# Vision-tower kernel: each half of the edge convolution in front of a value group, the second half of the keys one group later

## The chip, the cores and the metric

The kernel runs on one core of one Trainium2 chip. The metric is the device time of one execution in microseconds, the median of the runs. TensorE (PE) does matmuls and its own weight loads (PEld); VectorE (DVE), ScalarE (ACT) and GpSimd (POOL) do the elementwise work; SyncE's queue (SP) issues the DMAs. Each engine works through its own instructions in the order in which they are written, and semaphores hold it where it needs another's result.

## The reference

One transformer layer over 32 grey edge images of 256 rows; each row of an image is a token of 256 values, with a class token ahead (257 tokens). Cut to what matters:

```python
gray  = einsum('bchw,c->bhw', x, w)                       # 32 images 256x256
edge  = (|conv(gray, scharr_x)| + |conv(gray, scharr_y)|) / 2
h     = concat([cls, edge], axis=1)                       # 257 tokens
q,k,v = split(layernorm(h) @ w_qkv + b_qkv)               # 16 heads of 16
att   = softmax(where(causal, q @ k.T / 4, -inf))
h     = h + (att @ v) @ w_out + b_out
h     = h + fake_quant_ffn(layernorm(h))                  # 704 wide, gate and up, int8 style
```

The attention stage fills about the first 880 us, the feed-forward stage the rest. The change touches the attention stage only.

## The kernel before, in words

The attention stage is a software pipeline over images. Step n works on up to seven images at once: the grey sum of image n, the convolution, layer norm and transposes of image bC = n-2, the q, k, v projections of bP = n-3, the scores of bS = n-4, softmax and values of bT = n-5, and the output projection of bO = n-6. Steps 8 to 29 are a hardware loop in pairs; the others are written out. In every step each engine has one fixed order by hand; nothing else schedules. The names on PE, each a line of `step`:

- `scores(u)`, u = 0 to 7: scores of two heads into SX (L939, L942), so that DVE can take row maxima (`maxima`, L706 and L708). SX has one buffer, so `scores(u)` waits for the maxima of u-1.
- `scores_t(b, par, u)`: the scores again, transposed, into ST (L956); ACT takes the exponential into `prob` (L542).
- `outputs(b, par, g)`, g = 0 to 3: the value group, probabilities of four heads times v, into G (L975), in 32-column tiles. It waits for `sel_done`: POOL's `select` (L449, then the causal mask L451) on the same four heads.
- `edges(t)`, t = 0, 1: half of the convolution into the PSUM bank M1 (L994), also in 32-column tiles. ACT takes the absolute value (`absolute`, L572), DVE goes on (`edge_tile`, L734).
- `keys(m)` into M0 or M1 (L1007), `queries(m)` into M0 (L1018). ACT copies each result twice (L552 and L554, L563 and L565).
- `spread_rec` (L1055): spreads the reciprocals of the softmax sums over G. It waits for the DMA `rec<-den` (L375), which SP issues after the four `yun<-yun` DMAs.
- `turn_max`: turns the maxima into M1 (L1046); DVE copies them (L723), and a DMA brings them to `qst`.

POOL's step, for the part that matters (it is written once and the same before and after):

```python
select(bT, 1)
...                                   # L462, a small copy
wait(pool, kx_ready, bP, 4, 4)        # both halves of the keys copied by ACT
nc.gpsimd.tensor_tensor(kr, kx, kpart[0], subtract)       # L466
select(bT, 2)
...
```

So the selection for `outputs(2)` stands on POOL behind L466, and L466 waits for ACT's copies of `keys(1)`. Later in the same step stand L471 (keys), L475 (queries), L480 to L483 (layer norm) and `select(bT, 3)`, which `outputs(3)` needs.

Of the kernel before, what the change touches and what calls it, by code (L numbers as in the profile page):

```python
# [73 lines left out]
def vit_tower(nc, x, cls_tok, scharr, w_qkv, b_qkv, w_out, b_out, clip_x, clip_down,  # L74
# [8 lines left out]
    with ctx:  # L83
# [423 lines left out]
        def _(act):  # L507
# [22 lines left out]
            def step(n, par):  # L530
                bC, bP, bS, bT = n - 2, n - 3, n - 4, n - 5

                def exponential(b, u):
                    if valid(b):
                        g = u // 2
                        wait(act, sT_done, b, 8, u + 1)
                        if u % 2 == 0:
                            if g >= 2:
                                wait(act, pv_done, b, 4, g - 1)
                            else:  # L540
                                wait(act, pv_done, b - 1, 4, 3 + g)
                        nc.scalar.activation(prob[:, g % 2, 2 * (u % 2):2 * (u % 2) + 2, 0:QEND],  # L542
                                             ST[:, :, 0:QEND], ACT.Exp).then_inc(exp_done, 1)

                def keys(m):
                    if valid(bP):
                        wait(act, k_done, bP, 2, m + 1)
                        if m == 0:
                            wait(act, k_rest, bP - 1, 1, 1)
                            wait2(act, kst_loaded, bP - 1, par, 96)  # L550
                        bias = bqk[:, KC + m:KC + m + 1]
                        nc.scalar.activation(kpart[:, 0, m, 1:T], M[m][:, 0:IMG], ACT.Identity, bias=bias  # L552
                                             ).then_inc(kx_ready, 1)
                        nc.scalar.activation(kx[:, m, 1:T], M[m][:, 0:IMG], ACT.Identity, bias=bias  # L554
                                             ).then_inc(kx_ready, 1)

                def queries(m):
                    if valid(bP):
                        wait(act, q_done, bP, 2, m + 1)
                        if m == 0:  # L560
                            wait(act, q_rest, bP - 1, 1, 1)
                            wait2(act, qst_loaded, bP - 1, par, 96)
                        nc.scalar.activation(qpart[:, 0, m, :], M[0][:, 0:IMG], ACT.Identity,  # L563
                                             bias=bq4[:, m:m + 1], scale=HD ** -0.5).then_inc(qx_ready, 1)
                        nc.scalar.activation(qx[:, m, :], M[0][:, 0:IMG], ACT.Identity,  # L565
                                             bias=bq4[:, m:m + 1], scale=HD ** -0.5).then_inc(qx_ready, 1)

                def absolute(t):
                    if valid(bC):
                        wait(act, conv_done, bC, 2, t + 1)  # L570
                        wait(act, ln1, bC - 1, LN, 2 * t + 1)
                        nc.scalar.activation(habs[:, t, :, :], M[1][:, :].rearrange("p (f w) -> p f w", f=2),  # L572
                                             ACT.Abs, scale=0.5).then_inc(abs_done, 1)
# [7 lines left out]
                                       ).then_inc(yun_ready, 1)  # L581

                exponential(bT, 3)
                absolute(0)
                keys(0)
                exponential(bT, 4)
                keys(1)
                exponential(bT, 5)
                queries(0)
                absolute(1)  # L590
                exponential(bT, 6)
                if valid(bP):
                    wait(act, k_rest, bP, 1, 1)
                    nc.scalar.copy(kpart[:, 1, :, 1:T], kr[:, :, 1:T]).then_inc(k_mid, 1)  # L594
# [279 lines left out]
        def _(pe):  # L874
# [49 lines left out]
            def step(n, par):  # L924
# [20 lines left out]
                def scores_t(b, par_, u):  # L945
                    if valid(b):
                        if u >= 1:
                            wait(pe, exp_done, b, 8, u)
                        else:
                            wait(pe, exp_done, b - 1, 8, 8)  # L950
                        if u % 4 == 0:
                            wait(pe, m_loaded[u // 4], b, 16, 16)
                        for r in range(2):
                            i = 2 * u + r
                            for k in range(KT):
                                last = mm(ST[0:KEYS[k], r, QAT[k]:QAT[k] + QN[k]],  # L956
                                          kst[par_][:, i, KFIRST[k]:KFIRST[k] + KEYS[k]], qst[par_][:, i, Q0[k]:IMG],
                                          start=True, stop=True)
                        last.then_inc(sT_done, 1)

                def outputs(b, par_, g):
                    if valid(b):
                        wait(pe, sel_done, b, 4, g + 1)
                        if g % 2 == 0:
                            wait(pe, yun_ready, b - 1, 2, g // 2 + 1)
                        if g == 2:
                            wait(pe, yn_done, b - 1, 1, 1)
                        if g == 0:
                            wait2(pe, v_placed, b, par_, 16)
                            wait(pe, v_ready, b, 1, 1)  # L970
                            wait(pe, v_first, b, 2, 2)
                        for k in range(KT):
                            for j in range(4):
                                o = G[32 * j:32 * j + 32, g // 2, IMG * (g % 2) + Q0[k]:IMG * (g % 2) + IMG]
                                last = mm(o, vaug[par_][0:KEYS[k], k, head_at(4 * g + j), :],  # L975
                                          prob[0:KEYS[k], g % 2, j, QAT[k]:QAT[k] + QN[k]],
                                          start=k == 0, stop=k == KT - 1)
                        last.then_inc(pv_done, 1)

                def edges(t):  # L980
                    if valid(bC):
                        if t == 0:
                            wait(pe, gst_loaded, bC, 96, 96)
                            wait(pe, msplit, bT, 2, 2)
                            if ends:
                                wait(pe, v_first, bS, 2, 2)
                                wait(pe, abs_done, bC - 1, 2, 2)
                        else:
                            wait(pe, kx_ready, bP, 4, 4)
                            if ends:  # L990
                                wait(pe, abs_done, bC, 2, 1)
                        for f in range(2):
                            for j in range(4):
                                last = mm(M[1][32 * j:32 * j + 32, IMG * f:IMG * f + IMG], cw[:, f, :],  # L994
                                          gst[:, 4 * t + j, :], start=True, stop=True)
                        last.then_inc(conv_done, 1)

                def keys(m):
                    if valid(bP):
                        if m == 0:  # L1000
                            wait(pe, xT_ready, bP, 1, 1)
                        else:
                            wait(pe, abs_done, bC, 2, 1)
                            if ends:
                                wait(pe, msplit, bT, 2, 2)
                        for c in range(KC):
                            last = mm(M[m][:, 0:IMG], wqkv[:, c, D + P * m:D + P * m + P], xT[:, c, 1:T],  # L1007
                                      start=c == 0, stop=c == KC - 1)
                        last.then_inc(k_done, 1)
# [40 lines left out]
                def spread_rec():  # L1050
                    if valid(bO):
                        wait(pe, rec_moved, bO, 16, 16)
                        wait(pe, yun_ready, bO, 2, 2)
                        for c in range(KC):
                            last = mm(G[:, 1, IMG * c:IMG * c + IMG], sel[0:H, P * c:P * c + P],  # L1055
                                      rec[:, :], start=True, stop=True)
                        last.then_inc(rec_spread, 1)
# [28 lines left out]
                    pe.wait_ge(w_sd, 1)  # L1086
                scores(0)
                scores_t(bT, odd, 3)
                edges(0)
                keys(0)  # L1090
                scores(1)
                scores_t(bT, odd, 4)
                outputs(bT, odd, 1)
                keys(1)
                scores(2)
                scores_t(bT, odd, 5)
                spread_rec()
                queries(0)
                edges(1)
                scores(3)  # L1100
                scores_t(bT, odd, 6)
                outputs(bT, odd, 2)
                queries(1)
                turn_max(0)
# [546 lines left out]
```

## Time and profile before

| | us |
|---|---|
| median of 3 runs (1167.91 to 1173.79) | 1169.92 |
| the profiled execution | 1166.12 |
| its span in the trace | 1164.4 |
| PE busy | 949.2 |
| DVE busy | 806.9 |
| ACT busy | 686.8 |
| POOL busy | 537.5 |

The busy times are sums over the whole span. Two stages stand in it: up to about 880 us the attention pipeline, in which PE is busy 461.10 of the 500 us from 300 to 800, and then the feed-forward stage, in which DVE is the busiest. PE's granted clock is at its full level of 2.4 GHz in the first of these stretches (the profile's 1.00). A step of the pipeline is seen as the distance between two `edges(0)`.

### The profile page before, as it was taken

What the parts mean: (1) busy time and instruction counts of PE and PEld (TensorE: products, weight loads), DVE (VectorE), ACT (ScalarE), POOL (GpSimd) and SP (SyncE); (2) the same over time, 40 slices, a digit from 0 to 9 for tenths busy, and PEclk for the clock granted to TensorE, in tenths of its full rate; (3) what the DMA queues carried; (4) which work ended last, traced back from release to release, by engine and by line L of the source; (5) the groups of instructions that cost most, each with busy time, mean ns of one, the idle gap of its engine ahead of it and who ended that gap; (6) DMA issues with size and microseconds to landing.
All of it is one profiled execution on the core that took longest, in us unless ns stands there. A gap on an engine that the chain in (4) does not pass through costs nothing. (4 is left out here: it accounts for less than half of the span.)

```text
span 1164.4 us, 28062 instructions
## 1 busy us (share of the span) xinstructions
PE 949.2 (82%) x9584; PEld 681.1 (58%) x9584; DVE 806.9 (69%) x1969; ACT 686.8 (59%) x1171; POOL 537.5 (46%) x685
## 2 busy tenths in 40 slices
PE   2268899989989999899999999989988458885665
PEld 1045666666766767676676766767666333332544
DVE  1735566777776677777767777776666359998687
ACT  0154666666666666666666666666554237785785
POOL 5243555566556555655656565556443242220000
PEclk9988999999999999999999999999998769998888
DMA  3854455555555556555455655554322005501874
GB/s 86 233 133 112 126 138 152 149 133 148 149 133 129 137 154 150 138 150 143 126 135 148 154 135 150 148 131 105 101 62 62 12 1 199 199 1 50 271 231 137
DMA packets 156101, 152.90 MB, mean 131 GB/s; under 512 B 28263, under 2 KB 152458, under 8 KB 153994
## 3 DMA queue, kind: packets, MB, share of 16 engines
q1 hardware_dynamic: 156042, 152.14, 48.2%
q8 instruction: 34, 0.56, 0.2%
q14 instruction: 25, 0.20, 0.1%
HBM read 67.49 MB, written 28.35 MB: 82 GB/s over the span
## 5 line engine op out<-in xcount | busy, mean ns | idle before, releaser
L542 ACT ACTIVATE prob<-ST 128x772 f32<-128x772 f32 x256 | 209.2, 817 | 149.2 <-PE ST L956 143.9
L706 DVE TENSOR_REDUCE mneg<-SX 128x2 f32<-128x258 f32 x256 | 107.5, 420 | 212.3 <-PE SX L942 211.7
L939 PE MATMUL SX<-kst,qst 96*128 96x257 bf16 (+1 forms) x1024 | 159.9, 250 | 19.1 <-DMA qst<-qpart 10.4
L708 DVE TENSOR_REDUCE mneg<-SX 128x2 f32<-128x514 f32 x256 | 174.0, 680 | 0.0
L956 PE MATMUL ST<-qst,kst 98*128 98x256 bf16 (+2 forms) x1536 | 138.7, 223 | 15.5 <-DMA qst<-mpart 15.2
L942 PE MATMUL SX<-mask_s,ident_b 128*128 128x256 bf16 x512 | 142.4, 278 | 0.0
L451 POOL TENSOR_SCALAR_AFFINE_SELECT prob<-prob 128x1016 f32<-128x1016 f32 x128 | 142.2, 1111 | 0.0
L956 PEld LDWEIGHTS ST<-qst,kst 98*128 98x128 bf16 x1536 | 120.9, 99 | 33.8 <-DMA qst<-mpart 12.7
L939 PEld LDWEIGHTS SX<-kst,qst 96*128 96x128 bf16 x1024 | 91.7, 99 | 64.3 <-issue 28.2
L975 PE MATMUL G<-prob,vaug 128*32 128x256 f32 (+2 forms) x3072 | 117.3, 282 | 14.2 <-POOL prob L451 13.2
L975 PEld LDWEIGHTS G<-prob,vaug 128*32 128x32 f32 x3072 | 83.5, 111 | 48.1 <-POOL prob L451 19.7
L994 PE MATMUL M<-gst,cw 102*32 102x256 f32 x1024 | 71.1, 396 | 26.2 <-DMA gst<-gray_dram 17.1
L499 POOL TENSOR_TENSOR gray<-xin 128x512 f32<-128x512 f32 x32 | 40.5, 1267 | 90.4 <-ACT xin L620 90.4
L471 POOL TENSOR_TENSOR kpart<-kqr,kpart 128x512 bf16<-128x512 f32 x32 | 37.0, 1156 | 95.2 <-ACT kpart L594 95.2
L1368 ACT ACTIVATE work<-GU,gsc 128x512 f32<-128x512 f32 x96 | 65.4, 685 | 23.7 <-PE GU L1570 23.4
L1622 PE MATMUL GU<-wdT,hq 128*128 128x256 bf16 x384 | 54.5, 311 | 30.3 <-ACT hq L1396 30.3
L466 POOL TENSOR_TENSOR kqr<-kqr,kpart 128x512 f32<-128x512 f32 x32 | 37.0, 1157 | 86.0 <-ACT kqr L554 86.0
L449 POOL TENSOR_TENSOR tick<-half 128x2 f32<-128x2 f32 x128 | 29.9, 234 | 99.9 <-ACT prob L542 99.8
L1007 PE MATMUL M<-xT,wqkv 128*128 128x256 f32 x256 | 73.1, 409 | 0.0
L1570 PE MATMUL GU<-work,wgT 128*128 128x512 bf16 x192 | 58.5, 387 | 17.0 <-ACT work L1354 10.9
L1018 PE MATMUL M<-xT,wqkv 128*128 128x256 f32 x256 | 72.3, 404 | 0.0
L620 ACT ACTIVATE xin<-xin 128x512 f32<-128x512 f32 x96 | 53.1, 620 | 23.8 <-DMA xin<-in_x 23.8
(226 smaller groups left out, 1991.8 us busy)
## 6 DMA issues: line engine op xcount, KB each, us to landing
kst<-kpart SPq DMA_DIRECT2D x192, 128.5 KB, 2.5
xin<-in_x SPq DMA_DIRECT2D x96, 256.0 KB, 4.0
gst<-gray_dram SPq DMA_DIRECT2D x96, 256.0 KB
qst<-qpart SPq DMA_DIRECT2D x192, 128.0 KB, 2.4
h_dram<-hb SPq DMA_DIRECT2D x8, 1280.0 KB, 4.6
gray_dram<-gray SPq DMA_DIRECT2D x64, 128.0 KB, 2.7
result<-oy SPq DMA_DIRECT2D x32, 256.0 KB, 3.4
hb<-h_dram SPq DMA_DIRECT2D x5, 1280.0 KB, 6.5
```

Source lines behind the costliest of these rows:

```text
L451: nc.gpsimd.affine_select(p, p, [[0, 4], [-1, 2], [1, P - 1]], ALU.is_ge, 0.0, base=1, channel_multiplier=-1).then_inc(sel_done, 1)
L542: nc.scalar.activation(prob[:, g % 2, 2 * (u % 2):2 * (u % 2) + 2, 0:QEND], ST[:, :, 0:QEND], ACT.Exp).then_inc(exp_done, 1)
L706: nc.vector.tensor_reduce(mneg[:, 0, u // 4, 0, at], SX[:, :, S0:S0 + P + 1], AX.X, ALU.max, negate=True)
L708: nc.vector.tensor_reduce(mneg[:, 1, u // 4, 0, at], SX[:, :, S1:S1 + T], AX.X, ALU.max, negate=True).then_inc(max_done, 1)
L939: mm(SX[:, r, at:at + k], qst[par][0:SR, 2 * u + r, P * t:P * t + P], kst[par][0:SR, 2 * u + r, 0:k], start=t == 1, stop=False)
L942: last = mm(o, ident_b[:, :], mask_s[:, :, :], start=False, stop=True)
L956: last = mm(ST[0:KEYS[k], r, QAT[k]:QAT[k] + QN[k]], kst[par_][:, i, KFIRST[k]:KFIRST[k] + KEYS[k]], qst[par_][:, i, Q0[k]:IMG], start=Tru ...
L975: last = mm(o, vaug[par_][0:KEYS[k], k, head_at(4 * g + j), :], prob[0:KEYS[k], g % 2, j, QAT[k]:QAT[k] + QN[k]], start=k == 0, stop=k == ...
L994: last = mm(M[1][32 * j:32 * j + 32, IMG * f:IMG * f + IMG], cw[:, f, :], gst[:, 4 * t + j, :], start=True, stop=True)
L1007: last = mm(M[m][:, 0:IMG], wqkv[:, c, D + P * m:D + P * m + P], xT[:, c, 1:T], start=c == 0, stop=c == KC - 1)
L1018: last = mm(M[0][:, 0:IMG], wqkv[:, c, P * m:P * m + P], xT[:, c, 1:T], start=c == 0, stop=c == KC - 1)
L1368: nc.scalar.activation(silu[0:IW[k], j % NSI, :], GU[k % 3][0:IW[k], 0, :], ACT.Silu, scale=gsc[0:IW[k], k:k + 1]).then_inc(silu_done, 1)
```

## The change

On PE `edges(0)` goes from in front of `keys(0)` to in front of `outputs(1)`, `edges(1)` from behind `queries(0)` to in front of `outputs(2)`, and `keys(1)` from behind `outputs(1)` to behind `spread_rec`, in front of `queries(0)`. ACT's copies go into the matching order. POOL's, DVE's and SP's orders stay. The waits inside the functions stay too.

```diff
 # ACT
                 exponential(bT, 3)
-                absolute(0)
                 keys(0)
                 exponential(bT, 4)
+                absolute(0)
+                exponential(bT, 5)
                 keys(1)
-                exponential(bT, 5)
                 queries(0)
+                exponential(bT, 6)
                 absolute(1)
-                exponential(bT, 6)
 # PE
                 scores(0)
                 scores_t(bT, odd, 3)
-                edges(0)
                 keys(0)
                 scores(1)
                 scores_t(bT, odd, 4)
+                edges(0)
                 outputs(bT, odd, 1)
-                keys(1)
                 scores(2)
                 scores_t(bT, odd, 5)
                 spread_rec()
+                keys(1)
                 queries(0)
-                edges(1)
                 scores(3)
                 scores_t(bT, odd, 6)
+                edges(1)
                 outputs(bT, odd, 2)
                 queries(1)
                 turn_max(0)
```

PE before, in a step of the loop, from the end of `outputs(1)` (L975) over `keys(1)` (L1007) to `spread_rec` (L1055), `queries(0)` (L1018) and `edges(1)` (L994):

```order
L975 MATMUL G<-prob,vaug 32x1 x4
L1007 MATMUL M<-xT,wqkv 128x256 x2
L939 MATMUL SX<-kst,qst 128x257
...
L956 MATMUL ST<-qst,kst 128x1
L1055 MATMUL G<-rec,sel 128x256 x2
L1018 MATMUL M<-xT,wqkv 128x256 x2
L994 MATMUL M<-gst,cw 32x256 x8
L939 MATMUL SX<-kst,qst 128x257
```

PE now, in the same stretch of a step, from `edges(0)` and `outputs(1)` on:

```order
L994 MATMUL M<-gst,cw 32x256 x8
L975 MATMUL G<-prob,vaug 32x256 x4
L975 MATMUL G<-prob,vaug 32x129 x4
L975 MATMUL G<-prob,vaug 32x1 x4
L939 MATMUL SX<-kst,qst 128x257
...
L956 MATMUL ST<-qst,kst 128x1
L1055 MATMUL G<-rec,sel 128x256 x2
L1007 MATMUL M<-xT,wqkv 128x256 x2
L1018 MATMUL M<-xT,wqkv 128x256 x2
L939 MATMUL SX<-kst,qst 128x257
```

`keys(1)` has moved behind one `scores`, one `scores_t` and `spread_rec`; the convolution stands directly in front of the value group.

ACT before, in a step of the loop, from the copies of `keys(0)` (out of M0) on:

```order
L552 ACTIVATE kpart<-M0,bqk 128x256
L554 ACTIVATE kqr<-M0,bqk 128x256
L542 ACTIVATE prob<-ST 128x2x386
L552 ACTIVATE kpart<-M1,bqk 128x256
L554 ACTIVATE kqr<-M1,bqk 128x256
L542 ACTIVATE prob<-ST 128x2x386
L563 ACTIVATE qpart<-M0,bq4 128x256
L565 ACTIVATE kqr<-M0,bq4 128x256
L572 ACTIVATE habs<-M1 128x512
```

ACT now, in the same stretch:

```order
L552 ACTIVATE kpart<-M0,bqk 128x256
L554 ACTIVATE kqr<-M0,bqk 128x256
L542 ACTIVATE prob<-ST 128x2x386
L572 ACTIVATE habs<-M1 128x512
L542 ACTIVATE prob<-ST 128x2x386
L552 ACTIVATE kpart<-M1,bqk 128x256
L554 ACTIVATE kqr<-M1,bqk 128x256
L563 ACTIVATE qpart<-M0,bq4 128x256
L565 ACTIVATE kqr<-M0,bq4 128x256
```

The copies of `keys(1)` (out of M1) stand one exponential later, and directly in front of those of `queries(0)`.

## Rows read from the trace of the kernel before

**Rows 1.** The page, part 1: busy us (share of span) and instructions.

```profile
PE 949.2 (82%) x9584; PEld 681.1 (58%) x9584; DVE 806.9 (69%) x1969; ACT 686.8 (59%) x1171; POOL 537.5 (46%) x685
```

**Rows 2.** Waits of PE, 250 to 750 us: us in total, times, longest.

```profile
PE M L1046 <- DVE mneg L715: 11.8, 19, 0.8
PE G L975 <- POOL prob L451: 7.9, 18, 0.6
PE M L994 <- DVE mpart L723: 7.5, 19, 0.6
```

**Rows 3.** Timeline of PE, one step: start, us, line, tile, count [idle before, releaser].

```profile
399.60 0.53 PE L956 MATMUL ST<-qst,kst 98*128 98x256 bf16 x6
...
400.34 1.07 PE L994 MATMUL M<-gst,cw 102*32 102x256 f32 x16 [0.22 <-DVE mpart L723]
401.34 1.13 PE L1007 MATMUL M<-xT,wqkv 128*128 128x256 f32 x4
...
403.42 0.90 PE L975 MATMUL G<-prob,vaug 128*32 128x256 f32 x24
404.25 1.13 PE L1007 MATMUL M<-xT,wqkv 128*128 128x256 f32 x4
405.22 0.33 PE L939 MATMUL SX<-kst,qst 96*128 96x257 bf16 x2
...
405.78 0.53 PE L956 MATMUL ST<-qst,kst 98*128 98x256 bf16 x6
406.24 1.13 PE L1055 MATMUL G<-rec,sel 16*128 16x256 f32 x4
407.29 1.13 PE L1018 MATMUL M<-xT,wqkv 128*128 128x256 f32 x4
408.36 1.07 PE L994 MATMUL M<-gst,cw 102*32 102x256 f32 x16
...
410.39 0.90 PE L975 MATMUL G<-prob,vaug 128*32 128x256 f32 x24
...
417.62 0.90 PE L975 MATMUL G<-prob,vaug 128*32 128x256 f32 x24 [0.62 <-POOL prob L451]
...
426.12 1.07 PE L994 MATMUL M<-gst,cw 102*32 102x256 f32 x16 [0.58 <-DVE mpart L723]
```

**Rows 4.** Timeline of POOL in the same step.

```profile
399.53 1.27 POOL L499 TENSOR_TENSOR gray<-xin 128x512 f32<-128x512 f32 x1 [2.69 <-ACT xin L620]
...
402.25 1.11 POOL L451 TENSOR_SCALAR_AFFINE_SELECT prob<-prob 128x1016 f32<-128x1016 f32 x1
...
406.33 1.16 POOL L466 TENSOR_TENSOR kqr<-kqr,kpart 128x512 f32<-128x512 f32 x1 [2.27 <-ACT kqr L554]
...
407.78 1.11 POOL L451 TENSOR_SCALAR_AFFINE_SELECT prob<-prob 128x1016 f32<-128x1016 f32 x1
...
413.30 1.16 POOL L475 TENSOR_TENSOR qr<-kqr,qpart 128x512 f32<-128x512 f32 x1 [0.17 <-ACT kqr L565]
414.66 0.71 POOL L480 TENSOR_TENSOR rs<-ve,half 128x2 f32<-128x2 f32 x1 [0.20 <-DVE ve L748]
```

**Rows 5.** Timeline of ACT in the same step.

```profile
405.79 0.47 ACT L554 ACTIVATE kqr<-M,bqk 128x256 f32<-128x256 f32 x1
```

**Rows 6.** Timeline of SP's queue, in two steps of the loop and in a late one.

```profile
403.86 0.58 SPq L375 DMA_DIRECT2D rec<-den  x1
...
429.48 0.58 SPq L375 DMA_DIRECT2D rec<-den  x1
...
866.33 0.58 SPq L375 DMA_DIRECT2D rec<-den  x1
```

**Rows 7.** Timeline of PE in that late step.

```profile
868.23 1.13 PE L1055 MATMUL G<-rec,sel 16*128 16x256 f32 x4 [0.86 <-DMA rec<-den]
...
871.27 0.90 PE L975 MATMUL G<-prob,vaug 128*32 128x256 f32 x24
```

**Rows 8.** Timeline of DVE in the step of rows 3.

```profile
400.55 0.67 DVE L708 TENSOR_REDUCE mneg<-SX 128x2 f32<-128x514 f32 x1
```

## The prediction

> **What bounds the kernel now.** I read the page's busy times first [rows 1]: PE is the busiest engine at 82% of the span, but no engine is at its limit over the whole span. The next view was PE's waits in the middle of the attention stage [rows 2]. The reader is to see that they are short and many: each of the three largest comes about once in each of the 19 or so steps of that stretch, 0.4 to 0.6 us at a time. So a step is a ring of handovers in which PE is nearly always working and is held several times for a few tenths. In such a ring time taken out of PE counts only up to the next handover that is already tight, and time added to another engine's chain counts from where that chain's slack ends. So I followed one step through the timelines of PE, POOL, ACT and SP [rows 3 to 6]. It lasts 25.78 us, from `edges(0)` at 400.34 to the next at 426.12.
>
> Three handovers matter, in order.
>
> First, `outputs(1)` at 403.42. POOL's mask L451 started at 402.25 and took 1.11, so it ended at 403.36, and PE started 0.06 later. POOL had been at work without a pause worth the name since 399.53, when ACT's L620 released it [rows 3, 4]. So PE stood right at POOL's heel, and can't come earlier by being faster itself.
>
> Second, `outputs(2)` at 410.39. Its mask started at 407.78 and ended at 408.89, so there were 1.50 us between the end of the mask and its use, of which 0.06 are the handover: 1.44 us of slack. POOL had idled 2.27 us before L466, released by ACT's L554, the second copy of `keys(1)` [rows 3 to 5]. The chain is `keys(1)` on PE at 404.25, ACT's L554 from 405.79 to 406.26, POOL's L466 at 406.33, mask ended at 408.89, value group possible at 408.95. That is 4.70 us from the start of `keys(1)` to the earliest `outputs(2)`.
>
> Third, `outputs(3)` at 417.62, for which PE did idle 0.62 us on POOL. That POOL chain hangs on `queries(1)` and on `turn_max(0)`: L475 idled 0.17 for the copy of the queries and L480 0.20 for DVE's statistics, which follow the copy of the turned maxima [rows 3, 4]. Both stand behind `outputs(2)` on PE. So a delay of `outputs(2)` arrives at `outputs(3)` whole.
>
> **The change part by part.** No instruction is added or removed, and no wait. All costs are of position.
>
> `edges(0)` leaves the place in front of `keys(0)`. It held PE for 1.00 us (400.34 to 401.34), with 0.22 us idle in front in this step and 0.58 in the next, 7.5 us over 19 times [rows 2, 3]. That idle time goes, since by its new place DVE's copy has long been made. `keys(0)` would start 0.46 after the start of `scores_t` at 399.60 (the distance from 405.78 to 406.24), at 400.06, and `scores(1)` 0.97 later (the distance 404.25 to 405.22), at 401.03 [rows 3]. DVE's maxima of `scores(0)` end at 400.55 + 0.67 = 401.22 [rows 8], so here a new wait of 0.2 to 0.3 us is late next. Then come 0.56 for `scores(1)` (405.22 to 405.78), 0.46 for `scores_t`, `edges(0)` at about 402.3 and `outputs(1)` at the earliest at 403.2 to 403.4, depending on whether a convolution in front of a value group takes as little as a value group (0.83, from 403.42 to 404.25) or as much as now (1.00); no row shows that pair. In either case it is POOL's 403.36 that decides, and `outputs(1)` stays at 403.42. Gain so far: nothing.
>
> `keys(1)` leaves the place behind `outputs(1)`. `scores(2)` then starts at 403.42 + 0.83 = 404.25, `scores_t` at 404.81, and `spread_rec` could start at 405.27. It now started at 406.24. But the DMA that it waits for was issued at 403.86 in this step [rows 6]. How long this DMA takes to release PE is seen in the late step where PE did wait for it: issued at 866.33, `spread_rec` at 868.23, so 1.90 us [rows 6, 7]. That makes 405.76, a new wait of 0.49 us. The queue itself doesn't gain: its DMAs are released through DVE's copy of the maxima at the step's start, and SP's order is the old one. `keys(1)` follows 1.05 later (406.24 to 407.29), at 406.81 instead of 404.25. With the 4.70 us of the chain, `outputs(2)` can start at 411.51 instead of 410.39: 1.12 us later. In the following step the DMA is issued 25.62 us later (429.48) while the step is 25.78 long, so the loss there is 0.96. The two kinds of step alternate, and the mean is **1.04 us a step**.
>
> PE itself would not be late. `keys(1)` and `queries(0)` take 0.97 each, `scores(3)` 0.56, `scores_t` 0.46 and `edges(1)` 0.83 to 1.00, about 3.9 in all, so PE is ready for `outputs(2)` at 406.81 + 0.97 + 0.97 + 0.56 + 0.46 + about 0.9 = 410.7. It waits 0.8 us there for POOL. If the DMA doesn't hold `spread_rec`, `outputs(2)` is at 405.27 + 1.05 + 4.70 = 411.02, still 0.63 late; that is the lower bound of this term (0.47 in the other kind of step, mean 0.55). The upper bound is reached if ACT and POOL have to queue more than now: ACT's copies of `queries(0)` now follow directly behind those of `keys(1)`, and `absolute(1)` falls between the next exponential and the copy L594; none of these stands in front of L554, so I allow another 0.5 us, 1.5 in all.
>
> `edges(1)` moves behind `scores_t`. Its successors (the absolute value, DVE's `edge_tile`, then the copy of the turned maxima) have until `turn_max(0)`, two groups later, now also 1 us later. `edges(1)` at about 409.8 ends by 410.9, ACT's L572 behind it by 411.7, `turn_max(0)` comes at 411.51 + 0.83 + 0.97 = 413.31. I cost it at nothing; what hides it is `outputs(2)` and `queries(1)`.
>
> Switches between 32-column and 128-column groups get fewer. `queries(0)` in front of `edges(1)` takes 1.07 (407.29 to 408.36), `keys(1)` in front of `scores(2)` 0.97, so such a border costs about 0.10 [rows 3]. The Trainium skill ("TensorEngine Tiling (Array Packing)", Key Properties) says that changing the tiling mode drains the engine. The trace agrees with its 0.10 us at the border. Four borders a step go, since each half of the convolution now shares its way in and out with a value group: 0.4 us of PE's time a step. By that rule alone the kernel would get faster. I give the 0.4 us no value in the sum, because it lies in front of POOL's release at `outputs(1)` and at `outputs(2)`.
>
> **The sum.** Steps 6 to 33 have all stages, 28 in number: 28 x 1.04 = 29.1 us. In step 34 there is no convolution, but the keys move too: `spread_rec` at 868.23, `keys(1)` 1.05 later at 869.28, `outputs(2)` at 873.98 instead of 871.27 [rows 7], 2.7 us. Steps 3 to 5, where the weights are prepared, and the steps behind 34, which have no keys, I put at 0, with 3 us either way. The feed-forward stage isn't touched. Together +31.8 us. The profiled execution took 1166.1 (span 1164.4), so it would be 1197.9; it lay 3.8 us below the median of the runs, 1169.9, and with the same 31.8 the median is **1201.7**. A measurement of this kernel can tell about 0.5% (6 us) from no change, and this is 2.7%.
>
> **The rivals.**
> - PE sets the step, and the ring gives way (faster). Then the idle time at `edges(0)` (7.5 / 19 = 0.39 us) and the four borders (0.4) are gained: 0.8 x 28 = 22 us, 1148; with the borders alone 0.4 x 28 = 11 us, 1159. For it: PE's 82%. Against it: POOL's mask is tight at `outputs(1)` already, and the distance `keys(1)` to `outputs(2)` shrinks on PE while the chain through ACT and POOL keeps its length. It decides if the chain from `keys(1)` through ACT and POOL were shorter than PE's own 3.9 us between the two groups, and POOL released `outputs(1)` earlier. Chance 0.09. The case of the borders alone is the one of the Trainium skill's page named above.
> - The delay at `outputs(2)` is absorbed later, at the places where PE waits now (0.62 at `outputs(3)`, 0.6 at `turn_max(1)` by the row of L1046 [rows 2]). For it: the waits are there. Against it: they are chains that start at PE's own late groups. Time: 1170 plus what is left, 1166 to 1176. Chance 0.07.
> - The DMA holds nothing, only POOL's chain does: 28 x 0.55 + 2.7 = 18 us, 1188. Chance 0.17.
> - More is queued than I see (1.5 us a step): 28 x 1.5 + 2.7 = 45 us, 1215. Chance 0.12.
> - My forecast, both holds as worked out, 1201.7: chance 0.55.
>
> **How the numbers follow.** Faster by over 0.5%: 0.09. Within 0.5%: 0.07. Slower by over 0.5%: 0.55 + 0.17 + 0.12 = 0.84. The range takes in the forecast, the case without the DMA and most of the case above: 1182 to 1214.
>
> **What would show it.** Right: POOL's idle time before L466 grows from 2.3 to nearly 5 us; PE's waits show `outputs` on L451 with 0.8 us more a step (from 7.9 us in 500 to over 20), `spread_rec` on the `rec<-den` DMA with about 0.5 us a step, and a new short one of L939 on DVE's L708; the waits of L994 on L723 are gone; a step is about 26.8 us. Wrong: `outputs(2)` shows no idle time on POOL, or it does and the step is still 25.8 us or less, so that a later wait gave it back.

## The result and the profile after

| | before | after |
|---|---|---|
| median of 4 runs, us | 1171.86 | 1209.13 (1203.52 to 1216.36) |
| profiled execution, us (span) | 1166.12 (1164.4) | 1203.52 (1201.8) |

The ratio is 1.031, with a 95% interval of 1.026 to 1.036. The forecast was 1201.7 us, a ratio of 1.027.

The waits of PE between 250 and 750 us, in the kernel after (us in total, times, longest):

```profile
PE ST L956 <- DMA qst<-mpart: 19.1, 37, 1.2
PE M L1046 <- DVE mneg L715: 15.2, 18, 1.0
PE G L975 <- POOL prob L451: 13.0, 24, 0.6
PE SX L939 <- DVE mneg L708: 5.6, 18, 0.5
PE G L1055 <- DMA rec<-den: 2.8, 10, 0.3
```

In the kernel before, the first of these stood fourth, behind the three of [rows 2]:

```profile
PE ST L956 <- DMA qst<-mpart: 5.9, 18, 0.5
```

Against [rows 2] three things are to be seen. The wait of L994 on L723 is gone and a short one of L939 on L708 has come, both as forecast. POOL's mask is waited for longer, 13.0 instead of 7.9 us, but not the 20 and more that I expected. And the largest wait is one of which the prediction said nothing: `scores_t` on the DMA `qst<-mpart`, twice a step.

One step on PE, after (start, us; idle time before and its releaser in brackets):

```profile
412.56 0.54 PE L956 MATMUL ST<-qst,kst 98*128 98x256 bf16 x6 [0.27 <-DMA qst<-mpart]
413.03 1.07 PE L994 MATMUL M<-gst,cw 102*32 102x256 f32 x16
413.92 0.87 PE L975 MATMUL G<-prob,vaug 128*32 128x256 f32 x24
415.29 0.53 PE L956 MATMUL ST<-qst,kst 98*128 98x256 bf16 x6
416.12 1.12 PE L1055 MATMUL G<-rec,sel 16*128 16x256 f32 x4 [0.29 <-DMA rec<-den]
417.17 1.13 PE L1007 MATMUL M<-xT,wqkv 128*128 128x256 f32 x4
418.14 1.03 PE L1018 MATMUL M<-xT,wqkv 128*128 128x256 f32 x4
419.56 0.53 PE L956 MATMUL ST<-qst,kst 98*128 98x256 bf16 x6
420.02 1.07 PE L994 MATMUL M<-gst,cw 102*32 102x256 f32 x16
421.68 0.90 PE L975 MATMUL G<-prob,vaug 128*32 128x256 f32 x24 [0.58 <-POOL prob L451]
...
428.07 0.54 PE L956 MATMUL ST<-qst,kst 98*128 98x256 bf16 x6 [0.59 <-DMA qst<-mpart]
428.90 0.90 PE L975 MATMUL G<-prob,vaug 128*32 128x256 f32 x24 [0.29 <-POOL prob L451]
```

POOL in the same step, after:

```profile
419.25 1.16 POOL L466 TENSOR_TENSOR kqr<-kqr,kpart 128x512 f32<-128x512 f32 x1 [5.32 <-ACT kqr L554]
...
420.51 1.11 POOL L451 TENSOR_SCALAR_AFFINE_SELECT prob<-prob 128x1016 f32<-128x1016 f32 x1
```

SP's queue in the same step, after:

```profile
414.13 0.58 SPq L375 DMA_DIRECT2D rec<-den  x1
...
421.15 2.09 SPq L392 DMA_DIRECT2D gst<-gray_dram  x6
424.43 0.70 SPq L360 DMA_DIRECT2D qst<-mpart  x1
...
426.11 3.82 SPq L403 DMA_DIRECT2D kst<-kpart  x6
```

The forecast chain is there: L466 idles 5.32 us for the copies of `keys(1)` (2.27 in [rows 4]), the mask ends at 421.62 and `outputs(2)` starts 0.06 later after 0.58 us idle. Beside it stands the second thing: SP issues the `gst` loads only when `edges(1)` has ended (420.02 + 1.07, issue at 421.15), the small `mpart` DMA follows at 424.43, and `scores_t(bS, 0)` can start only at 428.07, 3.64 us after its issue.

To compare kernels I measured the start of each group of a step from the start of DVE's L723 in front of it (the copy for the second half of the maxima). These are medians over 10 to 20 steps of the loop, most between 300 and 760 us, worked out from the start times in each trace. Where two kinds of step alternate, other stretches give medians that differ by up to 0.2 us, and in the row of `edges(1)` alone by up to 0.5:

| us from L723 | spread_rec | edges(1) | outputs(2) | gst issued | mpart issued | scores_t(bS,0) | outputs(3) | step |
|---|---|---|---|---|---|---|---|---|
| before | 6.41 | 8.53 | 10.56 | 9.68 | 13.31 | 16.66 | 17.61 | 25.64 |
| after | 5.87 | 9.78 | 11.44 | 10.94 | 14.19 | 18.01 | 18.71 | 26.83 |
| keys(1) moved alone | 5.87 | 8.99 | 11.44 | 10.14 | 14.19 | 17.17 | 18.53 | 26.58 |
| both edges moved alone | 6.78 | 9.82 | 10.71 | 10.98 | 13.44 | 18.33 | 18.80 | 27.24 |
| edges(0) alone | 6.78 | 8.89 | 10.93 | 10.05 | 13.68 | 16.94 | 18.01 | 26.08 |
| edges(1) alone | 6.35 | 9.40 | 10.29 | 10.58 | 13.02 | 17.86 | 18.33 | 27.48 |
| after, small gst | 5.88 | 9.79 | 11.45 | 10.94 | 14.20 | 17.10 | 18.53 | 26.54 |
| after, select first | 5.88 | 9.79 | 10.67 | 10.94 | 13.40 | 18.51 | 18.98 | 27.40 |
| after, small gst and select first | 5.88 | 9.79 | 10.67 | 10.94 | 13.40 | 16.31 | 17.75 | 25.75 |

Where the 37.4 us between the two spans lie is seen from `spread_rec`: its first group (step 6), the one in step 34 and its last (step 37). Before, beside [rows 7], it stands at

```profile
147.23 1.13 PE L1055 MATMUL G<-rec,sel 16*128 16x256 f32 x4
...
931.28 2.07 PE L1055 MATMUL G<-rec,sel 16*128 16x256 f32 x4 [8.96 <-DMA rec<-den]
```

and after at

```profile
146.94 1.13 PE L1055 MATMUL G<-rec,sel 16*128 16x256 f32 x4 [0.42 <-DMA rec<-den]
...
901.10 1.13 PE L1055 MATMUL G<-rec,sel 16*128 16x256 f32 x4 [1.42 <-DMA rec<-den]
907.13 0.90 PE L975 MATMUL G<-prob,vaug 128*32 128x256 f32 x24 [0.38 <-POOL prob L451]
...
971.25 2.07 PE L1055 MATMUL G<-rec,sel 16*128 16x256 f32 x4 [8.96 <-DMA rec<-den]
```

From step 6 to step 34 it took 721.0 us before (147.23 to 868.23) and 754.2 after (146.94 to 901.10): 33.2 us more, 1.18 a step. From there to the last it took 63.1 before and 70.2 after, 7.1 more; the mean granted clock in these two stretches was 0.83 before and 0.75 after. All the rest is 2.9 us less.

### The profile page after: what moved, and what is told of

It is laid out like the page before. It is cut to its first block and busy times, and to the rows that moved or that the text cites. A ratio compares the mean times of both kernels' runs of the same rounds, so it can differ in the third digit from the quotient of the medians.

```text
span 1201.8 us, 28084 instructions
## 1 busy us (share of the span) xinstructions
PE 948.6 (79%) x9584; PEld 682.7 (57%) x9584; DVE 819.5 (68%) x1969; ACT 685.3 (57%) x1171; POOL 532.3 (44%) x685
## 5 line engine op out<-in xcount | busy, mean ns | idle before, releaser
L939 PE MATMUL SX<-kst,qst 96*128 96x257 bf16 (+1 forms) x1024 | 160.3, 251 | 24.2 <-DVE mneg L708 11.6
L708 DVE TENSOR_REDUCE mneg<-SX 128x2 f32<-128x514 f32 x256 | 173.9, 679 | 0.0
L956 PE MATMUL ST<-qst,kst 98*128 98x256 bf16 (+2 forms) x1536 | 139.0, 223 | 39.6 <-DMA qst<-mpart 39.3
L956 PEld LDWEIGHTS ST<-qst,kst 98*128 98x128 bf16 x1536 | 118.7, 99 | 63.7 <-DMA qst<-mpart 29.8
L451 POOL TENSOR_SCALAR_AFFINE_SELECT prob<-prob 128x1016 f32<-128x1016 f32 x128 | 142.3, 1112 | 0.0
L975 PE MATMUL G<-prob,vaug 128*32 128x256 f32 (+2 forms) x3072 | 116.8, 282 | 23.7 <-POOL prob L451 23.1
L975 PEld LDWEIGHTS G<-prob,vaug 128*32 128x32 f32 x3072 | 86.2, 112 | 72.1 <-POOL prob L451 40.6
L939 PEld LDWEIGHTS SX<-kst,qst 96*128 96x128 bf16 x1024 | 89.9, 99 | 63.9 <-DVE mneg L708 35.8
L466 POOL TENSOR_TENSOR kqr<-kqr,kpart 128x512 f32<-128x512 f32 x32 | 37.1, 1158 | 170.1 <-ACT kqr L554 170.1
L994 PE MATMUL M<-gst,cw 102*32 102x256 f32 x1024 | 71.0, 396 | 17.9 <-DMA gst<-gray_dram 17.1
L449 POOL TENSOR_TENSOR tick<-half 128x2 f32<-128x2 f32 x128 | 24.7, 193 | 111.9 <-ACT prob L542 111.8
L1007 PE MATMUL M<-xT,wqkv 128*128 128x256 f32 x256 | 73.2, 409 | 0.7 <-ACT habs L572 0.7
L1570 PE MATMUL GU<-work,wgT 128*128 128x512 bf16 x192 | 58.7, 388 | 16.9 <-ACT work L1354 10.9
L1018 PE MATMUL M<-xT,wqkv 128*128 128x256 f32 x256 | 70.0, 396 | 0.0
L1067 PE MATMUL M<-wop,yn 128*128 128x256 f32 x256 | 65.9, 403 | 0.8 <-DVE yn L818 0.8
```

The lines of the kernel that those rows point to most:

```text
L451: nc.gpsimd.affine_select(p, p, [[0, 4], [-1, 2], [1, P - 1]], ALU.is_ge, 0.0, base=1, channel_multiplier=-1).then_inc(sel_done, 1)
L708: nc.vector.tensor_reduce(mneg[:, 1, u // 4, 0, at], SX[:, :, S1:S1 + T], AX.X, ALU.max, negate=True).then_inc(max_done, 1)
L939: mm(SX[:, r, at:at + k], qst[par][0:SR, 2 * u + r, P * t:P * t + P], kst[par][0:SR, 2 * u + r, 0:k], start=t == 1, stop=False)
L956: last = mm(ST[0:KEYS[k], r, QAT[k]:QAT[k] + QN[k]], kst[par_][:, i, KFIRST[k]:KFIRST[k] + KEYS[k]], qst[par_][:, i, Q0[k]:IMG], start=Tru ...
L1018: last = mm(M[0][:, 0:IMG], wqkv[:, c, P * m:P * m + P], xT[:, c, 1:T], start=c == 0, stop=c == KC - 1)
```

## The experiments

Two theories stood after the result. **A**, the prediction's: `keys(1)` late, so ACT's copies, POOL's L466 and the selection behind it late, so `outputs(2)` and `outputs(3)` late. **B**: `edges(1)` late, so the `gst` loads late, so the small `mpart` DMA lands late because it runs into their transfers, so `scores_t(bS, 0)` is late. All ratios are to the kernel before, with the 95% interval.

**1. keys(1) alone** (on PE behind `spread_rec`; the convolution where it was)

```diff
                 outputs(bT, odd, 1)
-                keys(1)
                 ...
                 spread_rec()
+                keys(1)
                 queries(0)
```

> The other half alone: keys(1) behind spread_rec, the two halves of the convolution where they stood before (edges(0) in front of keys(0), edges(1) behind queries(0)). Theory A: outputs(2) waits for POOL's mask, 1.0 us a step are lost, ratio 1.022 to 1.028. Theory B: edges(1) is only 0.3 us later, which the slack takes, ratio 1.000 to 1.003.

Measured: 1.031 (1.024 to 1.038), 1207.72 us, a step of 26.58. PE's waits, 250 to 750 us:

```profile
PE G L975 <- POOL prob L451: 21.2, 37, 1.1
...
PE G L1055 <- DMA rec<-den: 6.5, 18, 0.6
...
PE ST L956 <- DMA qst<-mpart: 0.4, 1, 0.4
```

This is A as forecast: twice a step on POOL's mask, once on the `rec<-den` DMA, and nothing on `mpart` but one wait. In the profile 0.94 us a step come from it. The ratio is above the expected range and higher than 28 such steps make (26 us). The profiled run had a few longer steps too, up to 30.9 us, one of them with a granted clock of 0.50 from 231 to 236 us; in the kernel after no such stretch lies in the loop. So the times of this experiment and of the whole change are alike (1.031 both), though the usual step is 0.25 us shorter here: it is the steps and not the times that tell the two apart.

**2. Both halves of the convolution alone** (`keys(1)` stays)

> One half of the change alone: edges(0) and edges(1) in front of outputs(1) and outputs(2), but keys(1) stays behind outputs(1), with ACT's copies in the matching order. Theory A: outputs(2) is not late, ratio 0.99 to 1.00. Theory B: edges(1) is about 0.9 us later in the step than in the kernel before; of this 0.6 us was slack in front of outputs(3), so 0.15 to 0.3 us a step are lost, ratio 1.004 to 1.008, and scores_t(bS, 0) idles about 1 us a step on the mpart DMA. Rival C (fewer switches between 32-column and 128-column groups count): ratio 0.98 to 0.99.

Measured: 1.038 (1.032 to 1.045), 1219.18 us. That alone is slower than the whole change, and outside all three expected ranges. Theory B had the place right and its size far too small.

```profile
PE ST L956 <- DMA qst<-mpart: 38.0, 35, 2.2
```

**3. and 4. Each half of the convolution alone**

> Of the change only edges(0) in front of outputs(1) (and absolute(0) behind the exponential on ACT); edges(1) and keys(1) as in the kernel before. If theory B (late gst loads collide with the mpart and kst transfers) is the cause of the loss seen with the convolution's half alone, this costs almost nothing, since conv_done of edges(1), which releases the gst loads, moves by 0.2 us: ratio 1.000 to 1.008. If it is the convolution's nearness to the value group or edges(0) itself, a good part of that loss (1.0385) shows here.

> Of the change only edges(1) in front of outputs(2) (and absolute(1) behind the exponential on ACT). Theory B: SP issues the gst loads 0.8 to 0.9 us later, the step gets longer by 0.9 to 1.5 us, ratio 1.025 to 1.036, with over 1.5 us idle in front of scores_t(bS, 0). Otherwise 1.00.

Measured: `edges(0)` alone 1.008 (1.005 to 1.010), `edges(1)` alone 1.047 (1.041 to 1.052), more than B's expected 1.036. So it is `edges(1)`, which releases the `gst` loads, and neither the place of `edges(0)` nor the nearness to a value group. In `edges(1)` alone that group is 0.87 us later in the step and `scores_t(bS, 0)` 1.20 later.

That it loses more than with `edges(0)` moved too is not the DMA: in both `mpart` is issued 2.46 us after `gst`, and PE idles 1.79 us for it in the median. It is the clock. In `edges(1)` alone two kinds of step alternate for most of the loop, of 26.4 to 26.7 and of 28.0 to 28.2 us, and in the long ones the granted clock fell behind this idle time:

```profile
356.45 0.83 PE L956 MATMUL ST<-qst,kst 98*128 98x256 bf16 x6 [2.04 <-DMA qst<-mpart]
357.21 1.57 PE L975 MATMUL G<-prob,vaug 128*32 128x256 f32 x24
...
384.16 0.54 PE L956 MATMUL ST<-qst,kst 98*128 98x256 bf16 x6 [1.57 <-DMA qst<-mpart]
384.63 0.90 PE L975 MATMUL G<-prob,vaug 128*32 128x256 f32 x24
```

Over 250 to 750 us the mean granted clock was 0.96 in this kernel, 0.98 with both halves moved, and 1.00 before and after. A step lasted 27.57 us in the mean, 1.9 more than before. The steps at the full clock are about 0.9 longer than before; the rest, about 1 us, I estimate to be the lower clock's.

The 0.4 us of `edges(0)` alone come from `scores_t(bT, 4)`. With the 1.0 us of convolution no longer ahead of it, it waits for the other `mpart` DMA (0.27 us in the row at 412.56 of the kernel after), and `spread_rec` and all behind it are 0.37 later.

**5. The changed kernel with small gst loads** (the convolution then works on old data for seven of eight row groups)

```diff
+    some = GB if isinstance(n, int) and n < 5 else 1
-                  [[IMG + 2, k], [GR * (IMG + 2), GB], [1, IMG]])
+                  [[IMG + 2, k], [GR * (IMG + 2), some], [1, IMG]])
```

> The changed kernel with the gst loads cut to one of eight row groups from step 5 on (the convolution of the others works on old data): an eighth of their bytes, the same number of DMAs and waits. Theory A alone: the time of the changed kernel, ratio 1.030. Theory B in addition: the mpart DMA is no longer queued behind gst, scores_t(bS, 0) no longer idles (0.6 us now, over 1.1 in some steps), the long steps of 27 us go and all are about 26.6 us, 0.2 to 0.3 us a step less, ratio 1.023 to 1.026.

Measured: 1.025 (1.020 to 1.029), 1201.58 us, a step of 26.54. As expected with B, though the interval just touches that of the whole change (1.026 to 1.036). The waits (one line was added, so L957 is L956 and L976 is L975):

```profile
PE G L976 <- POOL prob L452: 28.6, 38, 1.1
...
PE ST L957 <- DMA qst<-mpart: 6.3, 19, 0.6
```

The 19 waits of L957 are those of `scores_t(bT, 4)`; `scores_t(bS, 0)` no longer waits for its DMA in any step. The order, the waits in the code and the number of DMAs are those of the changed kernel; the bytes alone took `scores_t(bS, 0)` from 18.01 to 17.10, and the step to that of `keys(1)` alone. The means over 250 to 750 us say the same: 26.85 for the whole change, 26.59 with small loads, 26.55 with `keys(1)` alone. So in the changed kernel A is 0.9 and B 0.3 us a step.

**6. The changed kernel, selection first**

```diff
                 # POOL
+                select(bT, 2)
                 if valid(bP):
                     wait(pool, kx_ready, bP, 4, 4)
                     ...                              # L466
-                select(bT, 2)
```

> The changed kernel with one edit on POOL: select(bT, 2) stands in front of L466 (the subtraction that waits for the copies of keys(1)), so outputs(2) no longer hangs on keys(1). Theory A (the chain keys(1), ACT, L466, select, outputs(2) sets the step): outputs(2) loses its 0.59 us of idle time and a step gets 0.5 to 0.6 us shorter, ratio to the kernel before about 1.017, 1190 us. Theory B (edges(1) is late, so SP issues the gst loads late, and the small mpart DMA queued behind them lands late, so scores_t(bS, 0) and outputs(3) are late): edges(1) stands in front of outputs(2) and does not move, so the step gains at most 0.15 us, ratio 1.027 to 1.031, and the idle time in front of scores_t(bS, 0) grows from 0.6 to about 1.2 us.

Measured: 1.045 (1.038 to 1.052), 1226.84 us. Slower still, which neither theory had. `outputs(2)` did come 0.77 earlier (10.67), and with it the turned maxima and `mpart`'s issue (13.40 instead of 14.19), yet `scores_t(bS, 0)` came 0.50 later. POOL is no longer among PE's waits, and this is:

```profile
PE ST L956 <- DMA qst<-mpart: 40.9, 36, 2.4
```

What decides is how long after the `gst` loads `mpart` is issued (medians, 250 to 750 us):

| | gst to mpart issued, us | mpart issued to scores_t(bS, 0), us |
|---|---|---|
| before | 3.63 | 3.37 |
| after | 3.27 | 3.76 |
| both edges moved, and edges(1) alone | 2.46 | 4.86 |
| after, select first | 2.46 | 5.07 |

The closer the small DMA follows the large loads, the longer it takes, and with an eighth of their bytes no step waits for it at either distance. A puts off `outputs(2)`, and with it `turn_max(0)` and `mpart`, and so keeps the DMA away from the loads: A's delay shields the kernel from B. That is why the two parts of the change don't add. The six `kst` loads come 1.68 us behind `mpart` in all of these kernels; what they add, these rows don't tell.

**7. Both causes away**

> The changed kernel with both suspected causes taken away: select(bT, 2) in front of L466, and the gst loads cut to one of eight row groups from step 5 on (the convolution of the others works on old data). The select edit alone lost time and the small loads alone gained 0.33 us a step. If the two causes (A, the chain from keys(1) through POOL; B, the mpart DMA behind the gst transfers) are the whole loss, the step is that of the kernel before or shorter: 25.3 to 25.7 us, ratio 0.990 to 1.003. If there is a third cause, such as PE's order itself, the ratio stays above 1.01.

Measured: 1.006 (1.003 to 1.009), 1183.07 us, a step of 25.75. The ratio is just above the range expected without a third cause, and far below the 1.031 of the change: the two causes account for all but 0.1 us a step. Of the 7 us that the ratio leaves, 28 such steps make 3; where the rest lies is not shown. That the step isn't shorter than before, with fewer switches on PE, goes with `outputs(3)`, for which PE waits on POOL every step:

```profile
PE G L976 <- POOL prob L452: 17.4, 19, 1.1
```

**8. The convolution alone, small gst**

> Both halves of the convolution moved, keys(1) in its old place, and the gst loads cut to one of eight row groups from step 5 on (the convolution of the others works on old data). Theory B: the loss of 1.6 us a step goes, ratio 0.997 to 1.006, against 1.0385 with the full loads. That it gets clearly faster than the kernel before I don't expect: outputs(3) hangs on POOL's chain behind queries(1).

Measured: 1.002 (0.999 to 1.005), a step of 25.79. Against 1.038 with the full loads, this is B once more, unshielded.

**9. to 11. The mpart DMA issued by ScalarE**

```diff
                 # SP
-                max_rows(bS, par, 0)
                 # ACT
                 exponential(bT, 7)
+                if valid(bS):
+                    wait(act, msplit, bS, 2, 1)
+                    act.dma_start(qst[par][SR:SR + 2, 0:8, :], mpart[0][:, :]).then_inc(m_loaded[0], 16)
```

> The changed kernel with the mpart DMA of scores_t(bS, 0) issued by ScalarE (behind exponential(bT, 7)) and not by SP behind the gst loads. If the small DMA is late because it is queued behind gst on SP's own queue, scores_t(bS, 0) no longer idles, step 26.5 us, ratio 1.021 to 1.026. If it is late because the DMA engines are busy with gst whoever issues it, the idle time stays at 0.6 to 0.7 us and the ratio at 1.030.

> The convolution's halves moved, keys(1) in its old place, and the mpart DMA issued by ScalarE. With SP's queue as the cause of the delay: the loss of the convolution's half goes (it was 1.6 us a step in the median), ratio 0.985 to 1.003, and this would be the best version. With busy DMA engines as the cause: as without the edit, 1.035 to 1.04.

> The changed kernel with select(bT, 2) in front of L466 and the mpart DMA issued by ScalarE. With SP's queue as the cause: both losses go, ratio 0.985 to 1.005. With busy DMA engines: about 1.045 as with the select edit alone.

Measured: 1.067 (1.060 to 1.073), 1.081 (1.076 to 1.086), 1.083 (1.078 to 1.089). All three are above both expected ranges: the DMA became later, not earlier or equal. In the first of them, on ACT, SP and PE:

```profile
413.69 0.62 ACTq L599 DMA_DIRECT2D qst<-mpart  x1
```

```profile
410.06 2.09 SPq L392 DMA_DIRECT2D gst<-gray_dram  x6
...
413.67 3.88 SPq L402 DMA_DIRECT2D kst<-kpart  x6
```

```profile
418.02 0.54 PE L958 MATMUL ST<-qst,kst 98*128 98x256 bf16 x6 [1.68 <-DMA qst<-mpart]
```

The edit changed more than the issuer. SP's `kst` loads no longer stand behind `mpart`, and go out in the same moment. The small DMA, 3.63 us behind `gst` as in the kernel before, releases PE after 4.33 us here and after 3.37 there. So the wait isn't cured by another queue, and the `kst` loads beside it cost about 1 us, if the issuer itself costs nothing; that no run separates. The Trainium skill ("DMA: Bandwidth & Descriptors", Issuing engines are not separate DMA queues) says that DMAs run on the same 16 engines and interleave, whichever engine issues them; these rows agree. The clock has a part in the three ratios as well: it was 0.97, 0.92 and 0.93 in the mean of 250 to 750 us.

**12. The kernel before, select(bT, 3) in front of the layer norm's L480 to L483 on POOL**

> The kernel before with one edit on POOL: select(bT, 3) stands in front of the layer norm's L480 to L483, which outputs(3) doesn't need. Its 0.62 us idle in front of outputs(3) should go until the wait of scores_t(bS, 0) on the mpart DMA (0.26 us) decides; layer norm's results are then 1.3 us later, still before ACT's L606. Step 25.2 us instead of 25.65, ratio 0.987 to 0.992. If a later handover takes it back: 1.00.

Measured: 1.004 (1.000 to 1.008), no gain. `outputs(3)` did come 0.50 earlier and the median step is 25.51, but the wait in front of `turn_max(1)` grew instead:

```profile
PE M L1046 <- DVE mneg L715: 18.9, 19, 1.0
```

against 11.8 in [rows 2], and five of the 22 steps between 200 and 800 us, in each of which the clock fell, took 26.9 to 27.2 us, which brings the mean to 25.9. Whether it would gain with a steady clock stays open. No version tried has a lower median time than the kernel before.

## Why the prediction was right, and where it was not

- *`outputs(1)` stays where it is.* Nearly: 3.80 instead of 3.59 us from L723. But not by POOL. `scores_t(bT, 4)` waits for an `mpart` DMA, a wait that had been covered by `edges(0)` and that I had not listed.
- *`spread_rec` waits for `rec<-den`, 1.90 us from its issue.* Right: 414.13 to 416.12 is 1.99. The wait is 0.3 and not 0.5 in this step, and comes in about every second one (10 times in 500 us), since PE comes later by the wait just named; `spread_rec` is 0.54 earlier than before, as worked out (405.76 against 406.24 is 0.48).
- *`keys(1)` to `outputs(2)` takes 4.70 us, `outputs(2)` is 1.04 late.* The chain is right and a little shorter: 417.17 to 421.68 is 4.51. Late by 0.88, shown by experiment 1. There it arrives whole at `outputs(3)` (0.92) and in the step (0.94). The 29.1 us of this term were in truth about 26. Only the sign in PE's waits was off in the whole change (13.0 us on L451, not over 20, which experiment 1 does show), since the wait for `mpart` takes the place of part of that for POOL in front of `outputs(3)`: 0.62 before, 0.29 after.
- *`edges(1)` moves, costed at nothing.* This step failed. I had followed its result through ACT and DVE and not through SP, although `conv_done` releases the `gst` loads there. It cost 0.3 us a step in the changed kernel (experiment 5) and 1.45 where A doesn't shield it (27.24 in experiment 2 against 25.79 in experiment 8, in medians, which a few steps at the lower clock hardly move). The working had the time of its end ("ends by 410.9"), which is when SP can issue the loads, some 1.3 us later than before, but I did not look at what they would collide with. Of the 0.3 about 0.2 is at `outputs(3)`; the rest comes behind it, where the wait for DVE's L715 is 15.2 us in 500 against 10.9 with small loads. Why it grows is not shown.
- *The borders, 0.4 us of PE a step.* Right in size: `edges(0)` takes 0.89 (413.03 to 413.92) instead of 1.00, and `queries(0)` 0.86 (418.14 to 419.56, less 0.56 for `scores(3)`) instead of 1.07. And right in worth: nothing, also with both causes away (experiment 7).
- *Step 34 costs 2.7.* 6.03 from `spread_rec` to `outputs(2)` (901.10 to 907.13) instead of 3.04: 3.0 us. Part of that is the clock, which was at 0.50 from about 902.7 to 906.1: `keys(1)` took 1.40 us of PE there and not 0.97. The steps behind lost 4.1 more, which I had put at 0. From step 34 to the last `spread_rec` the clock was at 0.50 for about 35 us after and 21 before (means of 0.75 and 0.83), so the lower clock can account for most of these 4.1; no run separates it.

So the sum of 31.8 came close to 37.4 with one term about 3 us too large and another, 8 us for B, left out. That B was so small was luck: A, which the prediction had right, kept the `mpart` DMA away from the late loads, and the prediction didn't know of either. Unshielded, B alone made the kernel slower (1.038) than the whole change did.

## What to carry to other kernels

For each group that moves, follow every semaphore that it raises, SP's DMAs first: a load that is released later collides with other transfers than before, and a small DMA on which the critical engine waits pays for it. A fixed in-order chain through other engines (here `keys(1)`, ACT, POOL, `outputs(2)`) needs its full length between its two ends; count that length before bringing the ends closer. Two delays in one ring can shield each other, so undoing one alone can make it worse. And before a loss is put down to a wait alone, compare the granted clock of the two kernels.

## What the runs showed of the hardware

TensorE's clock. In the kernel with both halves of the convolution moved alone, the step that holds 440 us took 29.9 us, 2.7 more than the median. PE had idled 2.04 us there, after a stretch at the full clock:

```profile
440.00 0.86 PE L956 MATMUL ST<-qst,kst 98*128 98x256 bf16 x6 [2.04 <-DMA qst<-mpart]
440.79 1.57 PE L975 MATMUL G<-prob,vaug 128*32 128x256 f32 x24
...
444.09 3.16 PE L1029 MATMUL M<-wqkv,xT 128*128 128x256 f32 x8
...
448.55 0.90 PE L975 MATMUL G<-prob,vaug 128*32 128x256 f32 x24
```

Busy time by stretch there (us, then each engine, then the granted clock, the DMA share and GB/s):

```profile
435.00:440.00 5.00, 2.82 (x19) 1.98 (x17) 4.36 (x9) 1.79 (x3) 4.67 (x7) 0.97 0.77 169
440.00:445.00 5.00, 5.00 (x44) 3.78 (x45) 1.41 (x5) 2.99 (x5) 0.45 (x1) 0.50 0.75 206
```

The granted clock is 0.50, the lower level of 1.2 GHz, for some 7 us after the wait; a value group takes 1.57 instead of 0.90 and the eight matmuls of L1029 3.16 instead of 1.97. The length of the wait alone doesn't tell when: in the same kernel's timeline the clock also fell at 606.9 us, behind 1.54 us idle, and did not at 690.1, behind 1.98. In `edges(1)` alone (experiment 4) it fell in about every second step, behind idle times near 2.0 us. So part of what the experiments with long waits lost, and of their spread, is this and not the wait itself.

DVE beside POOL. In the kernel after, a DVE cast of 128x16 elements (L713) took

```profile
420.82 0.83 DVE L713 CAST mtop<-mneg 128x16 bf16<-128x16 f32 x1
```

while POOL's mask ran from 420.51 to 421.62; it took 0.17 at 408.18, with POOL idle. It ended with the mask. So it was in each of the 19 steps between 250 and 750 us, while in the kernel before L713 never fell beside a long POOL instruction and took 0.17 to 0.18 each time. I had costed every DVE instruction at its duration before; PE did not wait for this one.
